# Decoder layer on one core: small products moved between the z projections, the v projections joined, and new portions for the 32 x 32 inverse

## The reference

```python
mixed = hidden_states @ w_qkv                 # q, k, v before the convolution
z = (hidden_states @ w_z).reshape(B, S, HV, DV)
mixed = silu(causal depthwise conv of 4 taps(mixed))
beta, g = sigmoid(b), -exp(A_log) * softplus(a + dt_bias)
def step(Sm, inp):
    q_, k_, v_, g_, b_ = inp
    Sm = Sm * jnp.exp(g_)[..., None, None]
    kv = jnp.einsum('bhk,bhkv->bhv', k_, Sm)
    delta = (v_ - kv) * b_[..., None]
    Sm = Sm + jnp.einsum('bhk,bhv->bhkv', k_, delta)
    o = jnp.einsum('bhk,bhkv->bhv', q_, Sm)
    return (Sm, o)
og = o * silu(z);  on = og * rsqrt(mean(og*og) + EPS) * norm_w;  out = on @ w_out
```

## Time and profile before

| | before |
|---|---|
| median of 3 runs | 2225.94 us (2223.59 to 2243.5) |
| the profiled execution | 2234.28 us, of which the span is 2232.4 us |
| PE / DVE / ACT / POOL busy in the span | 90% / 80% / 65% / 39% |
| mean granted TensorE clock | 0.965 |
| steady stretch, 237.00 to 1471.75 us | 13 groups of four ticks |

### The profile page before, as it was taken

One profiled execution on the slowest core, in us unless ns is written; L12 is line 12 of the kernel. 1 busy time (PEld: TensorE's weight loads), 2 busy tenths in 40 slices (PEclk: granted clock), 3 DMA queues, 4 the chain that ended last, 5 costly groups with the idle time before them and its releaser, 6 DMA issues.

```text
span 2232.4 us, 48707 instructions
## 1 busy us (share of the span) xinstructions
PE 2020.2 (90%) x18444; PEld 1603.0 (72%) x18444; DVE 1787.1 (80%) x3136; ACT 1458.0 (65%) x2819; POOL 872.1 (39%) x586
## 2 busy tenths in 40 slices
PE   4648999999999999999999999998876899999998
PEld 3436787878888788887887888776764467666777
DVE  6789898998989989898898988976335777767765
ACT  4545766778777676776777777764766656565632
POOL 1623444354443544443444444421343123313232
PEclk8869999999999999999999999998999999999999
DMA  3422322333233323322233223121252021222232
GB/s 77 95 70 54 78 43 73 74 63 71 59 73 71 67 65 65 71 64 65 72 61 78 43 75 83 39 50 43 55 178 88 1 79 64 104 95 76 88 138 87
DMA packets 274629, 161.52 MB, mean 72 GB/s; under 512 B 209352, under 2 KB 246752, under 8 KB 269280
## 3 DMA queue, kind: packets, MB, share of 16 engines
q1 hardware_dynamic: 274400, 158.41, 27.5%
HBM read 122.43 MB, written 35.91 MB: 71 GB/s over the span
## 4 chain that ended last, share of the span: by engine, by line
PE 54%; DVE 26%; issue 7%; ACT 6%; DMA 3%; SPq 3%; POOL 2%; DVEq 0%; ACTq 0%; POOLq 0%
PE ps L1412 9%; PE ps L1414 7%; PE ps L1413 7%; DVE A L952 7%; PE ps L1798 4%; PE ps L1578 4%; PE ps L1543 4%; DVE BP L1164 3%; DVE TM L1012 3%; PE ps L1660 2%; PE ps L1682 2%; PE ps L1564 2%; ACT SC L899 2%; DVE UT L1000 2%; DVE TI L1016 2%
## 5 line engine op out<-in xcount | busy, mean ns | idle before, releaser
L952 DVE SCALAR_TENSOR_TENSOR A<-ps,CW,A 128x508 f32<-128x508 f32 (+2 forms) x768 | 515.1, 733 | 39.6 <-ACT A L705 37.2
L1412 PE MATMUL ps<-XH,WH 128*128 128x512 f32 x768 | 344.3, 448 | 70.4 <-DVE A L952 68.7
L523 POOL TENSOR_TENSOR EB<-EB,HJ 128x1024 f32<-128x1024 f32 x64 | 123.0, 1922 | 617.5 <-DMA EB<-decay_rows 617.5
L1413 PE MATMUL ps<-XL,WH 128*128 128x512 f32 x768 | 311.2, 405 | 0.0
L1414 PE MATMUL ps<-XH,WL 128*128 128x512 f32 x768 | 311.1, 405 | 0.0
L1543 PE MATMUL ps<-WO,SZ 128*128 128x256 f32 x1024 | 246.6, 386 | 17.5 <-ACT Q L718 9.3
L1412 PEld LDWEIGHTS ps<-XH,WH 128*128 128x128 f32 x768 | 150.7, 196 | 117.8 <-DVE A L952 61.8
L1543 PEld LDWEIGHTS ps<-WO,SZ 128*128 128x128 f32 x1024 | 195.0, 193 | 52.3 <-issue 16.3
L507 POOL TENSOR_TENSOR Y<-Y,DL 128x1024 f32<-128x1024 f32 x62 | 146.8, 2367 | 109.1 <-ACT DL L718 109.0
L899 ACT ACTIVATE SC<-ps,A 128x128 f32<-128x128 f32 x512 | 141.9, 384 | 59.1 <-DVE A L1317 58.4
L1414 PEld LDWEIGHTS ps<-XH,WL 128*128 128x128 f32 x768 | 150.1, 195 | 35.8
(11 more groups left out here) (217 smaller groups left out, 4740.7 us busy)
## 6 DMA issues: line engine op xcount, KB each, us to landing
EB<-decay_rows SPq DMA_DIRECT2D x128, 256.0 KB, 4.7
WE<-expert_halves SPq DMA_DIRECT2D x32, 1024.0 KB, 5.1
x_blocks<-BP SPq DMA_DIRECT2D x256, 32.0 KB, 1.6
X<-x_blocks SPq DMA_DIRECT2D x16, 512.0 KB, 5.0
tt_blocks<-TI SPq DMA_DIRECT2D x16, 512.0 KB, 2.6
tn_blocks<-TM SPq DMA_DIRECT2D x16, 512.0 KB, 2.6
TTF<-tt_blocks SPq DMA_DIRECT2D x256, 32.0 KB, 4.1
expert_halves<-BP SPq DMA_DIRECT2D x8, 1024.0 KB, 5.6
```

Source lines behind the costliest of these rows:

```text
L952: dve.scalar_tensor_tensor(acc, ps(i, 0, [[128, 4], [1, 128 - s]]), at(CW, tile * 4 + 3 - s, [[1, 1]]), acc, ALU.mult, ALU.add).then_inc(s ...
L1412: pe.matmul(out, sa, ma, start=(kt == 0), stop=False)
L1413: pe.matmul(out, sa, mb, start=False, stop=False)
```

## The change

PE's order is altered in each tick with a v part: u1 moves ahead of z half 1, and v half 0 moves behind t64 and `norms_tr`, next to v half 1. The room of one `pump` is altered in ticks 8 to 63: 3000 instead of 1500 in the first tick of a group, 3000 instead of 4300 in the second and third, 5000 instead of 4300 in the fourth.

```diff
@@ DVE
-                    pump((1500 if n % 4 == 0 else 4300) if EARLY <= n < NSTEP else 0 if n == NSTEP else 5000 // rate)
+                    pump((5000 if n % 4 == 3 else 3000) if EARLY <= n < NSTEP else 0 if n == NSTEP else 5000 // rate)
@@ PE
                     if s4:
                         og_sums(k)
-                    if s3:
-                        z_proj(m, 1)
-                    if s4:
-                        og_sums_tr(k)
                     if sv:
                         pe.wait_ge(sem["ld_ta"], 48 * (vn + 1))
...
                         t.then_inc(sem["u1"], 1)
-                    if sv:
-                        v_proj(vn, 0)
+                    if s3:
+                        z_proj(m, 1)
+                    if s4:
+                        og_sums_tr(k)
                     if sv:
                         pe.wait_ge(sem["ld_tt"], 64 * (vn + 1))
                         pe.wait_ge(sem["u1_sb"], 2 * vn + 2)
...
                     if n % 4 == 0 and 4 <= n <= NSTEP:
                         norms_tr(n // 4 - 1)
                     if sv:
+                        v_proj(vn, 0)
                         v_proj(vn, 1)
```

## The result

The changed kernel takes 2267.17 us (median of 3 runs, 2267.17 to 2268.13) against 2225.94 us: a ratio of 1.017, with a 95% interval of 1.0145 to 1.0201 (this and the ratios below are estimated from all the runs of both kernels; the quotient of the two medians is 1.0185). The profiled execution of after has a span of 2265.3 us and a mean granted clock of 0.956, 32.9 us more than the span of before. The thirteen steady groups take 1265.49 us, 97.35 each, where they took 1234.75. So 30.7 us of the 32.9 lie there; the start is 0.6 us and the tail 1.6 us longer.

What follows compares the result with a forecast made beforehand. PE's own work was taken as the bound, 90.4 of 94.98 us a group, the rest waits. Eight groups at 96.9 and five at 99.2 us add 36 us to the 2226 median: 2262 us, range 2205 to 2285.

Steps and rivals of the forecast that it cites:

- The stretching: DVE's small products ahead of first-tick v taps wait for POOL's running large products: delay 6.4 us, taps at +28.1.
- The rival without stretching: 64-column products run at 0.2 us beside POOL; taps at +23.2, a group 93.6 to 94.1 us, about 2211; chance 0.25.
- The TTF stall: With v half 0 moved, PE waits for TTF loads: 1.7 us on average, about 22 us in 12 groups.
- the one on the fourth tick: DVE's idle time in the fourth tick (15.91 us busy of 23.02) covers the 0.7 us more room; costed at nothing.
- branch B: Clock drops at the TTF stall, eight of thirteen groups; POOL's L507 starts late, taps at +25.7, group 96.9 us.
- branch A: Clock held at the stall, five groups; taps at +28.1, clock drop at q/k projection, L1461 at +44.1, group 99.2 us.
- The gate: In first ticks DVE's gate starts 13.0 us behind the taps, against 11.7 before.
- The floor: PE is busy 22.61 us in a stage without waits, set by its own work; 4 x 22.6 = 90.4 a group.
- The relief in the second tick: The second tick loses 2.8 us of inverse ahead of its taps, so its 1.3 us wait goes.
- The heavier collisions: All groups in branch A: 2281; two 512-column L996 also meet L523, up to 1.9 us a group: 2306; chance 0.17.
- The loads in time: Last TTF load lands at +15.9, stall and clock drop vanish; with no stretching 92.0 us a group, about 2187; chance 0.08.

Runs made afterwards that it cites:

- the two runs with added instructions: Kernel before plus four two-input products of 64 columns ahead of first-tick v taps: 2281.73 us (1.0205); with four one-input reduces instead: 2240.08 us (1.0021).
- the run with the room behind the taps: Changed kernel, the first tick's extra 1500 ns of room moved from ahead of the v taps to behind the last: 2272.04 us, ratio 1.0171.
- the PE edit alone: Kernel before with PE's new order only, the inverse in its old portions: 2225.65 us against 2236.9, ratio 0.9947.
- the run with the third tick at 4300: Changed kernel with the third tick's room set back from 3000 to 4300: 2261.16 us against 2236.9, ratio 1.012.
- the portions alone: Kernel before with only the new pump rooms, PE in its old order: 2292.58 us against 2236.9, ratio 1.0266.
- the last run: PE's new order, old portions, SP's fourth-tick order rows, TTF, X stores; first tick's room 0 ahead of the v taps, 2200 behind: 2243.67 us, ratio 1.0028.
- the run with rows and TTF first: Kernel before with PE's new order, old portions, and SP's fourth-tick queue as decay rows, TTF, stores of X: 2213.24 us against 2233.64, ratio 0.9895.

## Why the prediction was right, and where its steps were not

The time (2262 predicted, 2267 measured) and the sign hold, and so does the main mechanism. That the time came so close is in part luck: all thirteen groups went the dearer way where I had put five (+18 us), and that way was 1.85 us a group cheaper than I had it (-24 us). In the profiled spans the change is +33 us where +36 was predicted; in the medians it is +41; the three runs of before had a low median (on other chips it ran at 2234 to 2238).

**The stretching** was right, in place and size. Four products of two SBUF inputs stand beside L596, L492 and L507, and the taps begin at +27.8 (predicted +28.1) and the q/k projection at +33.6 (+33.9). That the new shape behaves as the small ones do was the open point; the two runs with added instructions settle it. One detail was off: mostly one of the four is held, by L507, and L1012 ahead of them takes up L596 and L492. The sum is the same, since POOL's timetable sets the end. The rival without stretching was priced too low: the run with the room behind the taps has no stretched L996 of 64 columns and takes 97.06 us a group, not 93.6 to 94.1: L1461 starts at +40.4 on average instead of +38.5, and with the clock drop there the next tick follows 11.9 us later instead of 9.9.

**The TTF stall** was right for the PE edit alone (19.5 us against 22) and wrong for the change as a whole (2.5 us). The step that failed is the one on the fourth tick: "in the fourth DVE has ample idle time ... which covers the 0.7 us more room there", costed at nothing. That idle time, 15.91 us busy of 23.02, lies behind the taps; ahead of them DVE had 0.55 us. And what stands ahead grew by 2.8 us, not 0.7. The smaller room of the third tick leaves the L1035 of 768 columns (1.1 us) to the fourth, and so the L1035 of 1024 columns comes later and meets POOL. In before it started half a microsecond ahead of L596:

```profile
1088.87 1.23 DVE L1035 TENSOR_TENSOR TM<-TI,UT 128x1024 f32<-128x1024 f32 x1
```

In after it starts just behind L596 and is held (DVE, then POOL):

```profile
1011.04 2.89 DVE L1035 TENSOR_TENSOR TM<-TI,UT 128x1024 f32<-128x1024 f32 x1
1013.96 1.91 DVE L1041 TENSOR_REDUCE TI<-TM 128x64 f32<-128x1024 f32 x1
1015.80 2.68 DVE L952 SCALAR_TENSOR_TENSOR A<-ps,CW,A 128x508 f32<-128x508 f32 x4
```

```profile
1010.96 1.89 POOL L596 TENSOR_TENSOR Q<-A 128x1024 f32<-128x1024 f32 x1
1012.98 2.09 POOL L492 TENSOR_TENSOR WL<-WR,WH 128x512 fp32r<-128x512 f32 x1
```

It takes 2.88 to 2.89 us in each of the thirteen groups, and 1.23 in before and in the run with the third tick at 4300. The taps start at +0.8 on average instead of -1.3. So it is the prediction's own mechanism, at a place where I had not looked for it. PE's wait behind it, in the same tick:

```profile
1021.67 0.47 PE L1412 MATMUL ps<-XH,WH 128*128 128x512 f32 x1 [0.93 <-DVE A L952]
```

So PE waits 0.73 to 1.42 us at the fourth tick's q/k projection, 11.2 us in all, and reaches the TTF products at +16.8 to +17.6 instead of +15.9. The loads also land 0.9 us earlier on average (+16.7 against +17.6, the means of the thirteen landings of either kernel; the last of the four is issued at +13.1 on average in both, and 4.1 us to landing is the median in the group shown against 4.8). This comes with the inverse's work in the fourth tick too: the three runs that have it there land at +16.7 to +17.05 (this one, the portions alone, the room behind the taps), those that haven't, with the old SP order, at +17.4 to +17.7. By what way, no run here settles.

**The clock and the two branches.** With no stall there was no drop behind it, and so branch B, put at eight of thirteen groups, never came. Its share was too high in any case: where the stall is there, it was followed by a drop in 4 of 13 groups (PE edit alone) and in 5 (third tick at 4300). All groups went the way of branch A. That alone would have given 2281, but A was over-sized: a group was to take 99.2 us and took 97.35. The stage of the drop was read from one at a clock of 0.88, as 2.7 us. In the group shown the drop is this (the stretch's clock is 0.50, one of the two levels, 1.2 GHz):

```profile
1048.13:1051.54 3.41, 3.03 (x7) 2.46 (x8) 3.31 (x11) 2.03 (x3) 0.00 (x0) 0.50 0.41 78
```

At full clock this work takes half as long, so I put the price at 1.6 us. In eight groups it lasts 3.41 us, in five 6.83 (their means are 97.0 and 97.9 us), 61.4 us in all against 23.9 before. With the portions alone, where every group has a wait of 4.0 to 5.1 us and a drop of 6.83, a group takes 99.0 us. L1461 then starts at +42.6 (1057.53) instead of +44.1, and the next tick 9.7 us later, at +52.3 (+54.0).

**The gate** started 12.8 us behind the taps (1055.54), 13.0 predicted.

**The floor** of 22.6 us was taken as fixed. A third tick without waits takes 22.71 us in before, 22.59 with the portions alone, 22.5 with the PE edit alone and 22.39 in after. I had costed the order of the matmuls at nothing; it gives 0.2 us a tick, 10 us in the steady stretch. The portions give 0.1 us more, and no run shows why.

**The relief in the second tick** was right, but I had missed a part of it. In the second tick of before (start, duration, DVE and POOL):

```profile
1135.53 2.77 DVE L1012 TENSOR_TENSOR TM<-TI,UT 128x512 f32<-128x512 f32 x2
```

```profile
1135.13 1.89 POOL L596 TENSOR_TENSOR Q<-A 128x1024 f32<-128x1024 f32 x1
```

and of after:

```profile
1060.91 1.41 DVE L1012 TENSOR_TENSOR TM<-TI,UT 128x512 f32<-128x512 f32 x2
```

```profile
1063.06 1.89 POOL L596 TENSOR_TENSOR Q<-A 128x1024 f32<-128x1024 f32 x1
```

The first of the pair had run into POOL's squares in each of the thirteen groups, 1.36 us each time. I had not looked for this in the second tick. The place ahead of the taps has lost this collision beside the 2.8 us that were moved. Either is more than the wait of 1.0 to 1.3 us, and no run separates them.

**The rivals.** No stretching is refuted by the trace. The heavier collisions (L996 of 512 columns beside L523) did not occur in after, but they did in the last run, in 8 of 13 groups (in two more L527's step, line 530 there, held one for 0.35 us), where the work stood 2 us later than in the calm groups of before. What did occur in after is the one of L1035 above. The loads in time did come about in effect (10 of 13 groups without a wait for TTF), by another way than that rival's, and didn't bring its gain, since the taps had become the bound.

## What to carry to other kernels

Ahead of work on which the bottleneck engine waits, instructions with two SBUF inputs on VectorE should not stand where GpSimd runs a row of large tensor_tensor instructions: each can cost a whole one of them, and the length of a small one says nothing of the price. Moving them is not enough by itself, as the run with the room behind the taps shows: the amount ahead of the next wait counts as well, and so does the clock behind that wait. Idle time of an engine covers an addition only if it lies ahead of the instruction that is waited for; a share of busy time by stage doesn't show that. And where a stall goes, look for its next holder in the same queue: here rows, TTF and X took turns, and moving the loads gained some 0.5% (0.9947 to 0.9895, measured on two chips, with intervals that just touch) where the stall had cost its stage 2.1 us a group, 1.2% of the whole.

## What the runs showed of the hardware

A copy with one SBUF input was held too: L974, 128x32, took 1.93 us at 1015.11, and up to 1.65 in the run with rows and TTF first, against 0.2 where nothing held it; it ended with L596 each time. The reduces never were. The holding goes the other way too: L492 took 2.09 us at 1012.98 against 1.27 at 1037.50, since L1035 was running, which had started before it. A held product ends soon behind its holder, a small one within 0.1 us: a product of 512 columns (0.69 us alone) ended 0.55 us behind L596 or L526 (L523 of before), the L1035 of 1024 (1.23 alone) 1.08 behind. POOL's powers (L579 of 8 columns, L614 of 16) are listed as tensor_tensor instructions and last up to 2.9 us, but held nothing: in after, three L996 ran at 0.22 us beside L614, and so did these beside L579 (DVE, then POOL):

```profile
1035.05 0.42 DVE L996 TENSOR_TENSOR TM<-X,TI 128x32 f32<-128x32 f32 x2
```

```profile
1034.02 1.65 POOL L579 TENSOR_TENSOR SM<-SM 128x8 f32<-128x8 f32 x1
```

They move 8 or 16 columns where L596 and L507 move 1024. Whether that amount is what counts, no run here varied alone.
